# Folding the last weight row of each expert by accumulating transfers instead of VectorE operations, in a block of mLSTM and routed experts

## The reference, cut to what matters

```python
x = L0_attn_x                                  # 16 x 256 x 128
xn = _layernorm(x)
s = _L0_attn_ref(xn, ...)                      # mLSTM: decay matrix times q k^T, times v, head norm
g = _silu(_L0_ffn_ref(xn, ...))                # 8 experts, each token takes the one with the largest logit
x = x + s * g
# in _L0_ffn_ref, for each expert i:
h = xn @ w1[i] + b1[i]                         # w1: 8 x 128 x 1024
a, g = jnp.split(h, 2, axis=-1)
y = (a * jax.nn.sigmoid(g)) @ w2[i] + b2[i]    # kept where top1 == i
```

## Time and profile before

| what | value |
|---|---|
| median of 3 runs | 240.93 us (239.75 to 241.77) |
| the profiled execution's own time | 240.99 us |
| its span, first to last instruction | 239.2 us |
| mean granted TensorE clock | 0.975 |

### The profile page before, as it was taken

How to read it: one execution, slowest core, us unless ns; L and a number is a source line. 1 busy time by engine, 2 the same in 40 slices (tenths; PEclk the granted TensorE clock), 3 DMA queues, 4 the chain that set the end, 5 groups by cost and what they waited for, 6 DMA issues and landing times.

```text
span 239.2 us, 6066 instructions
## 1 busy us (share of the span) xinstructions
PE 209.1 (87%) x1824; PEld 170.8 (71%) x1832; DVE 181.8 (76%) x505; ACT 136.5 (57%) x313; POOL 100.0 (42%) x128
## 2 busy tenths in 40 slices
PE   0688879689999999979999999999999999999650
PEld 0568744335555555559999999999999999986310
DVE  6997378299989986648777988898889789671490
ACT  0276756779788796754555555555555655540110
POOL 7553200027777776000333364425533464366150
PEclk9988999999999999999999999999999999999975
DMA  6999999501441111401097021102101000000994
GB/s 175 266 419 418 282 299 394 221 3 46 146 137 53 49 53 59 115 21 33 15 261 204 26 58 52 55 22 62 44 30 50 28 25 25 26 11 13 251 315 137
DMA packets 29730, 29.30 MB, mean 122 GB/s; under 512 B 3295, under 2 KB 24807, under 8 KB 29697
## 3 DMA queue, kind: packets, MB, share of 16 engines
q1 hardware_dynamic: 26258, 24.59, 33.0%
q0 software_dynamic: 2272, 4.22, 5.4%
q10 hardware_dynamic: 1168, 0.10, 0.4%
HBM read 20.01 MB, written 9.34 MB: 123 GB/s over the span
## 4 chain that ended last, share of the span: by engine, by line
PE 67%; DVE 11%; issue 6%; ACT 5%; DMA 5%; DVEq 1%; SPq 1%; POOL 1%; ACTq 0%; POOLq 0%
PE bank L1195 13%; PE head_bank L1195 13%; PE bank L1204 12%; PE head_bank L1159 5%; PE bank L1169 5%; PE bank L1149 4%; PE head_bank L1052 4%; PE bank L1180 3%; PE bank L1148 3%; DMA xw<-y_tokens 2%; DVE stats L696 2%; PE bank L1037 2%; PE bank L1082 2%; DVE cm L859 2%; PE head_bank L1131 1%
## 5 line engine op out<-in xcount | busy, mean ns | idle before, releaser
L449 POOL DMA_INDIRECT y_tokens<-ffn,idx x39 | 39.2, 1004 | 76.3 <-DVE ffn L992 74.0
L443 POOL DMA_INDIRECT xs_sorted<-xw,pos x32 | 33.0, 1031 | 36.3 <-DVE pos L831 26.9
L1204 PE MATMUL bank<-w_sb,dm 128*128 x312 | 41.3, 275 | 0.5 <-DVE dm L976 0.5
L1195 PE MATMUL bank<-xsT,wc 128*128 128x128 f32 x320 | 39.3, 276 | 0.1
L1204 PEld LDWEIGHTS bank<-w_sb,dm 128*128 128x128 f32 x312 | 38.0, 192 | 0.7 <-issue 0.7
L1195 PEld LDWEIGHTS bank<-xsT,wc 128*128 128x128 f32 x320 | 37.4, 192 | 0.5 <-DVE wc L851 0.3
L1195 PE MATMUL head_bank<-xsT,wc 128*128 128x128 f32 x304 | 37.0, 275 | 0.0
L1195 PEld LDWEIGHTS head_bank<-xsT,wc 128*128 128x128 f32 x304 | 35.4, 192 | 0.0
L859 DVE TENSOR_TENSOR cm<-dm,head_bank 128x1024 f32<-128x1024 f32 (+1 forms) x32 | 29.0, 948 | 6.3 <-ACT dm L586 3.5
L600 ACT ACTIVATE wc<-w_sb 128x512 f32 x39 | 24.6, 630 | 14.3 <-issue 14.3
L586 ACT ACTIVATE dm<-bank 128x512 f32<-128x512 f32 x48 | 26.9, 594 | 4.5 <-PE bank L1149 3.5
(11 more groups left out here) (199 smaller groups left out, 352.0 us busy)
## 6 DMA issues: line engine op xcount, KB each, us to landing
x_sb<-in_L_attn_x SPq DMA_DIRECT2D x16, 256.0 KB, 5.1
w_sb<-in_L_ffn_w SPq DMA_DIRECT2D x8, 512.0 KB, 8.2
wc<-in_L_ffn_w SPq DMA_DIRECT2D x5, 512.0 KB, 17.1
xs_sb<-xs_sorted SPq DMA_DIRECT2D x13, 193.5 KB, 2.8
xs_sorted<-b_sb SPq DMA_DIRECT2D x1, 2048.0 KB, 17.3
xw<-y_tokens SPq DMA_DIRECT2D x8, 256.0 KB, 4.6
out_x<-xw SPq DMA_DIRECT2D x8, 256.0 KB, 3.6
y_tokens<-ffn,idx POOLq DMA_INDIRECT x39, 2.3
```

What stands on the lines that cost most here:

```text
L443: pool.indirect_dma_start(xs_dram, bass.IndirectOffsetOnAxis(ap=pos[:, t:t + 1], axis=0), xw[:, t, :], None).then_inc(s_scat, 16)
L449: pool.indirect_dma_start(y_dram, bass.IndirectOffsetOnAxis(ap=idx[:, j:j + 1], axis=0), ys_sb[:, j // CH % 2, j % CH, :], None, bounds_ch ...
L1195: last = pe.matmul(bank[2 * (j % 2) + k][:, c * P:(c + 1) * P], wc[:, j % 3, m:m + P], xsT[:, j % 2, :], start=True, stop=True)
L1204: last = pe.matmul(bank[6 + j % 2][:, 0:D], uT[:, j % 2, c, :], w2_sb[:, bass.ds(e * (HC * D) + c * D, D)], start=(c == 0), stop=(c == HC ...
```

## The change

The sixteen DVE subtractions, `FOLDS`, the eight repeated loads on SP and the scratch tile `row_x` go. In their place:

- ACT issues an eleventh small transfer after `gamma`: the last rows of the eight experts, 8x1024, into `wc[0:8, 0, :]` (32 KB). After its dummy square root and ahead of `rsqrt_start(0)` ACT waits for it, multiplies it by -1, waits for that, and issues its store to a DRAM tensor `negated_rows`.
- POOL, after its last prologue operation (L435) and ahead of the scatters, waits for that store and for all of w1, and issues eight transfers that read one negated row repeated over 127 partitions and add it to rows 0 to 126 of `w1_sb`. `s_sub` now counts 16 for each.
- The block tables take one step a batch in batches 1 to 9 (eight steps in all) instead of three.

```diff
@@ SP
-            for e in range(6):
-                sp.dma_start(last_row[e], w1[e, D - 1:D, :].partition_broadcast(P)).then_inc(s_bc[e], 16)
...
-            for e in range(6, E):
-                sp.wait_ge(s_sub, e - 5)
-                sp.dma_start(last_row[e], w1[e, D - 1:D, :].partition_broadcast(P)).then_inc(s_bc[e], 16)
-
-            sp.wait_ge(s_sub, 5)
             sp.wait_ge(s_scat, 16 * T)
@@ POOL
             pool.tensor_scalar(gamma[:, :], gamma[:, :], 1.0, None, ALU.add).then_inc(s_gamma, 1)
 
+            pool.wait_ge(s_nr, 16)
+            pool.wait_ge(s_w1, 16 * E)
+            for e in range(E):
+                pool.dma_start(w1_sb[0:P - 1, e, :], nrow_dram[e:e + 1, :].partition_broadcast(P - 1),
+                               accum_op=ALU.add).then_inc(s_sub, 16)
+
             pool.wait_ge(s_id, 1)
@@ ACT
             act.dma_start(gamma[:, :], ln_w.partition_broadcast(P)).then_inc(s_small, 16)
+            act.dma_start(last_rows, w1[:, D - 1, :]).then_inc(s_lr, 16)
...
             act.activation(spare[:, 0:1], zeros[:, 0:1], ACT.Sqrt).then_inc(s_dummy, 1)
+            act.wait_ge(s_lr, 16)
+            act.activation(last_rows, last_rows, ACT.Copy, scale=-1.0).then_inc(s_neg, 1)
+            act.wait_ge(s_neg, 1)
+            act.dma_start(nrow_dram, last_rows).then_inc(s_nr, 16)
             rsqrt_start(0)
...
-                    act.wait_ge(s_sub, E)
+                    act.wait_ge(s_sub, 16 * E)
@@ DVE, attention()
-                    if 1 <= b < 4:
-                        for _ in range(3):
-                            step_of = next(blocks, None)
-                            if step_of is not None:
-                                link(step_of)
-                    for _ in range(FOLDS.get(b, 0)):
-                        fold_half(folded[0])
-                        folded[0] += 1
+                    if 1 <= b < 10:
+                        step_of = next(blocks, None)
+                        if step_of is not None:
+                            link(step_of)
                     if b == B - 4:
-                        dve.wait_ge(s_sub, E)
+                        dve.wait_ge(s_sub, 16 * E)
```

More of the change, by code:

```diff
@@ L55, in mlstm_moe_block @@
     SCAT_AT = [t * 14 // T for t in range(T)]
-    FOLDS = {1: 1, 2: 1, 3: 1, 4: 1, 5: 2, 6: 2, 7: 2, 8: 2, 9: 2, 10: 2}
     GT = 8
@@ L65, in mlstm_moe_block @@
     y_dram = nc.dram_tensor("y_tokens", (NTOK, D), F32).ap()
+    nrow_dram = nc.dram_tensor("negated_rows", (E, H2), F32).ap()
     x_t = x.rearrange("b (k p) d -> p (b k) d", p=P)
@@ L89, in mlstm_moe_block @@
         xs_sb = sb("xs_sb", [P, NX, CH, DW])
-        row_x = sb("row_x", [P, H2])
         ident = sb("ident", [P, P])
@@ L182, in mlstm_moe_block @@
         uT = dflat[:, 2 * HID:4 * HID].rearrange("p (i c t) -> p i c t", i=2, c=HC)
-        last_row = [wc[:, 0, :], wc[:, 1, :], wc[:, 2, :], row_x[:, :],
-                    xs_sb[:, :, :, :].rearrange("p i n d -> p (i n d)")[:, 0:H2], ffn[:, 0:H2], wc[:, 0, :], wc[:, 1, :]]
+        last_rows = wc[0:E, 0, :]
         natbd = dflat[:, 0:3 * P].rearrange("p (n m) -> p n m", n=3)
@@ L205, in mlstm_moe_block @@
         s_b1 = sem("s_b1")
-        s_bc = [sem(f"s_bc{e}") for e in range(E)]
+        s_lr = sem("s_lr")
+        s_neg = sem("s_neg")
+        s_nr = sem("s_nr")
         s_sub = sem("s_sub")
@@ L868, in attention @@
                 blocks = experts_of_blocks()
-                folded = [0]
                 for b in range(B):
@@ L891, in attention @@
                 outputs(B - 1)
[L892 to L900, removed]
             def normalise(g):
```

## The result

The changed kernel takes 244.97 us (244.69 to 246.11, 4 runs) beside 240.80 for the kernel before (4 runs). The ratio is 1.0183, with a 95% interval of 1.0129 to 1.0237. The profiled execution took 244.69 us with a span of 242.6 and a mean clock of 0.975, against 240.99, 239.2 and 0.975: 3.7 us in its own time, 3.4 in its span.

A forecast was written before the change was run, and what follows sets the result against it. PE, busy 87% of the span, was taken as the bound, with DVE the bound in the prologue. 240.99 + 3.3 (wait on ACT) - 0.5 (tables) = 243.8 us, range 240.9 to 247.0.

The forecast's parts named there:

- PE bounds attention, folds lie beside it: Attention: PE sets 3.55 us a batch, so removing 11.0 us of DVE folds gains 0 to 0.4 us.
- Tables, -0.5 us: Early attention batches: one table step a batch removes their excess of 0.56 us; taken as -0.5 us, bounds 0 to 1.0.
- The wait on ACT, +3.3 us: Prologue: ACT's wait for the last rows delays the square roots, DVE and PE's third group; +3.3 us, bounds 0.6 to 5.6.
- The gap of 1.05 us: Prologue: DVE's one idle gap, before 19.48, absorbs 1.05 of its 4.2 us delay, leaving 3.15.
- The extra 0.1 to 0.2 for ScalarE's late share: Prologue, third group: 0.1 to 0.2 us more delay since ACT's share now starts behind its copies.
- Broadcasts and accumulations, 0: Removing eight SP broadcasts gains 0; eight accumulating POOL transfers cost 0, taking 15 to 45 us of 68 available.
- the deadline: The accumulations must end before DVE's weight copy, expected at 96.8 us.
- The sum: Whole kernel: 240.99 + 3.3 - 0.5 = 243.8 us, own range 242.9 to 245.0.
- nothing of the change acts in the loop: Expert loop: PE is busy 101.9 of 102 us there, so its length stays the same.
- The early landing: Rival, prologue: the last rows land in 3.1 us, shift only 0.6, time 240.8 us; chance 0.12.
- The clock fell a second time: Rival, before PE's third group: idle PE drops its clock again, about 1.6 us more, 245.4 us; chance 0.20.
- The late accumulations: Rival, DVE's weight copies: one engine per transfer makes accumulations say 12 us late, 256 us; chance 0.12.

The follow-up runs named there:

- e4: The kernel before without the sixteen subtractions and the eight broadcasts, tables still three steps a batch; ratio 0.9956, 252.04 us.
- e2: The kernel before with ACT's load of the last rows, wait, negation and store added ahead of the square roots, result unread; ratio 1.0164, 256.98 us.
- e11: The changed kernel with ACT's wait, negation and store moved behind the first two square roots; ratio 0.9994, 254.03 us.
- e10: The changed kernel, unchanged, run again on the chip of the last group; ratio 1.0186, 257.37 us.
- e6: The changed kernel with the load of the last rows issued ahead of the three biases and gamma, wait left in place; ratio 1.0047, 255.29 us.
- e8: The changed kernel without the eight accumulating transfers; load, wait, negation and store stay; ratio 1.0165.
- e1: The changed kernel with ACT's wait, negation and store moved behind the first two square roots, first run of this edit; ratio 1.0064.
- e5: The changed kernel with ACT's wait, negation and store moved behind the first two square roots, run on another chip; ratio 1.0106.
- e12: The changed kernel without the eight accumulating transfers, run again on the chip of the last group; ratio 1.0152.
- e7: The changed kernel with the tables back at three steps a batch in batches 1 to 3; ratio 1.0152.
- e3: The kernel before with one table step a batch in batches 1 to 9, folds and broadcasts kept; ratio 0.9979.
- e9: The kernel before, unchanged, profiled on the chip of the last group; 253.69 us.

## Why the prediction was right

*PE bounds attention, folds lie beside it.* Right: 11 us of folds gone (9.2 by the page's busy time), and the steady beat stayed 28.36 us for 8 batches. e4 values folds and broadcasts together at 0.4%, about 1.1 us and more than the 0 to 0.4 us of the bounds, on chips where VectorE has a stop to catch up after.

*Tables, -0.5 us.* Right by the first pair of profiles: 11.21 became 10.70. The experiments could not confirm it. That the folds' share in the early batches was nothing is not shown either.

*The wait on ACT, +3.3 us.* The mechanism is shown from three sides: added alone it makes the kernel before slower (e2), moved by a few lines it disappears when the rows have landed in time (e11 against e10), and it shrinks with an earlier load (e6). Its size was 2.5 us. The landing was 10.85 (11.2 predicted), the negation 1.06 (1.07), but the store's issue took 0.31 instead of 0.45 and VectorE went on at 12.60 instead of 13.15. The gap of 1.05 us was used up as said. The extra 0.1 to 0.2 for ScalarE's late share did not appear. That the landing came so near to `gamma`'s 5.6 us is in part luck: over ten profiles the same 32 KB took 3.94 to 7.20 us. Nor did the place in the queue hold it back: the three bias loads and `gamma`, which were issued ahead and share a semaphore, were all done only at 11.3 in the changed kernel, behind the rows at 10.85, and at 12.9 against 10.96 in e8.

*Broadcasts and accumulations, 0.* Right for the prologue and the deadline. The last issue starts at 32.05 and its transfer landed 26.6 us later, at 58.7, with the copy at 96.04, so 37 us were left. Their issue, 7.24 us in all, is a little under the 8 to 10 that came from the scatters' rows.

*The sum.* 243.8 predicted, 244.69 in the profiled execution, 244.97 as median. The terms I had make 2.0 by measurement (2.5 - 0.5), not 2.8. What brings it back up are two that I had at zero: 0.5 us in the expert loop and 0.9 at the end. So the total is near for a reason that the forecast didn't have, and that nearness is luck: an overestimate of 0.8 in the wait and 1.4 left out. I had said that nothing of the change acts in the loop, and that step failed: the loop takes 0.5 us more in the changed kernel and in each of e1, e5, e6, e8, e10, e11 and e12, though not in e7. e11 has it with the prologue on time, so the shift doesn't cause it, and e8 and e12 have it without accumulations. What e7 alone of the changed kernels lacks is the new order of the tables; that points to this order, on one profile of e7, and doesn't show it. e3 loses 0.66 us at the second of the two places and e2 0.61 at the first, against 0.36 before; how the order of the tables reaches the loop is open. The 0.9 at the end is within what that stretch varies by: from the last first-layer matmul to the end it was 27.5 us in e9, 28.5 in e10, 28.2 in e11 and 27.2 in e12.

*The rivals.* The early landing did not happen, and e6 shows what it would have given. The clock fell a second time in one execution of one kernel, e7, and cost 1.53 us there; its longer low stretch in the changed kernel cost nothing. The late accumulations did not happen. In the windows of e10 from 40 to 52 us, in which e12 shows that nothing but the accumulations runs, the mean share of the 16 engines is 1.06 to 1.08: eight transfers on one engine each would have filled half of them. The Trainium skill, page "DMA: Bandwidth & Descriptors", section "Why a DMA increments its semaphore by 16 and not by 1", has both, one engine for 127 partitions and an exception for some software-issued copies; these transfers went by the exception. They landed 9.0 to 26.6 us after their issue in the profile of the changed kernel.

## What to carry to other kernels

Work put on an idle engine is free only behind what the others wait for, and only if it ends before that engine's next work: the same four lines cost 3 us ahead of two 0.2 us square roots and nothing behind them in e5 and e11, in a queue that was idle for 4 us right there; in e1, with a later landing, they cost more than 1 us there too. The small load behind ten others took 3.9 to 7.2 us to land beside the first big loads, though it is 32 KB, so a wait for it belongs as late as its result allows, and its price is a range. And taking 11 us off an engine that is busy 76% of the time moved the end by half a microsecond (profiles of the first pair, with the tables) to about one (e4), because the beat was another engine's.

## What the runs showed of the hardware that I had not expected

Eight accumulating transfers of 508 KB, with a source row repeated over 127 partitions, were issued by POOL in 7.24 us, 0.9 us each, about as fast as scatters of 128 rows (0.97), and landed after 9.0 to 26.6 us (median 18.2). Beside them b2's plain load of 512 KB took 17.5 us to land in e10; in e12 on the same chip, without them, it took 6.8.

The same program took 240.8 us on one chip and 253.7 on others, most of it (9.8 of the 11.7 us by which e9's span is longer) in a stop at one place of the program, in which two engines of the core waited for nothing that the profile names. Ratios to before within a group held to 0.3% to 0.7%; a change of half a microsecond can't be seen through it.
